# Quantised attention: the maxima lead the exponentials by 18 blocks in place of 24

## The chip, the cores and the metric

The program runs on one NeuronCore of a Trainium2 chip. The metric is the device time of one execution in microseconds. One core has five engines that run their own instruction streams in order and meet by semaphores: TensorE (PE; its weight loads are listed apart as PEld), VectorE (DVE), ScalarE (ACT), GpSimd (POOL) and SyncE (SP), which starts the DMA transfers.

## The reference

Two layers over 2048 tokens of width 256: an attention with quantised operands, a mixture of 32 experts, a time-mixing scan, and a mixture of 8 experts. The change touches the first attention only. It has 16 heads of width 16, and every one of the 2048 queries looks at all 2048 keys:

```python
q = _fq_sym(q, axis=-1)
k = _fq_sym(k, axis=-1)
v = _fq_sym(v, axis=2)
attn = jnp.einsum('bhqd,bhkd->bhqk', q, k)
attn = jax.nn.softmax(attn.astype(jnp.float32), axis=-1)
attn = _fq_unsigned(attn, axis=-1)          # rounded to 0..255 steps of the row's maximum
out = jnp.einsum('bhqk,bhkd->bhqd', attn, v)
```

Because the weights are rounded to 255 steps of the row's largest one, the kernel needs the maximum of every row of scores before it can take that row's exponentials.

## The kernel before

The queries are cut into 16 tiles of 128. A tile and a head make one "head" n of 256 in the kernel's counting (`n = 16 t + h`). The scores of a head (128 x 2048) are computed twice: once for the maxima, in four **blocks** of 512 columns (1024 blocks in all, `fill_maxima`, L219), and once for the exponentials, in two **units** of 1024 columns (512 units, `fill_unit`, L233). The work of one head passes through the engines so:

- PE computes its blocks into PSUM banks 0 to 2 (L219). Block b may be written when the reduction of block b - 3 has emptied its bank. DVE takes the maxima (`top`, L425), two blocks and one block in turn, so three blocks are two reductions and six blocks are four.
- After the last block of a **group** of four heads, and one further reduction, DVE joins the maxima of the group (`shift`, L429), and POOL turns them into the biases of these four heads (L519 and L521, `make_biases`).
- PE computes the head's two units (L233); ACT takes the exponentials to bytes (L484), with the head's bias. PE waits until the unit two before has been read.
- SP transposes the bytes by DMA (L512); POOL widens them to bf16 (`weight`, the CAST at L536, one for each head, three buffers).
- PE multiplies them with the values: 16 small matmuls for each head (`sum_values`, L251), the first of which waits for that head's CAST.

The instruction streams are written out by loops. What ties the stages is the order on PE and on POOL. In each turn of PE's loop (`attention_tensor`, L295) stand 6 blocks, 3 units (one and a half heads) and three calls of `sum_values` for up to 9 of its matmuls each. `LEAD` is how many blocks are computed ahead of that loop, so block 24 + 6 i is the first of turn i, and unit 3 i likewise. The sums of head m start when the units of head m + 4 have been issued (one head later for the first head of a tile):

```python
if m >= NHEAD or u < NUNIT and m + BEHIND + (2 if h == 0 else 1) > u // 2:
    return step
```

On POOL the biases of a group stand in front of a CAST: those for heads n + 5 to n + 8 are made just ahead of the CAST of head n, for n = 3, 7, 11 and so on (62 times, n = 3 to 247):

```python
if n % 4 == 3 and n // 4 + 3 < len(group_of):
    make_biases(po, n // 4 + 3)
po.wait_ge(s_turn[n % 3], 16 * (n // 3 + 1))
```

The group of heads n + 5 to n + 8 ends with block 4 n + 35. Before a tile's outputs are taken (`finish_tile`, L412 and L415), DVE waits for the sums of its last head; where this stands among the reductions follows from `LEAD` too (`tile_end`).

Of the kernel before, what the change touches and what calls it, by code (L numbers as in the profile page):

```python
# [25 lines left out]
def program(nc, a, out, stop=None):  # L26
# [30 lines left out]
    with ExitStack() as whole:  # L57
# [9 lines left out]
        def flat(b0, b1):  # L67

            return bank[:, b0:b1, :].rearrange("p b n -> p (b n)")
# [75 lines left out]
        with ExitStack() as attention:  # L145
# [7 lines left out]
            NBLOCK = NTOK // 512  # L153
# [12 lines left out]

            LN255 = float(np.log(255.0))
            LOGS, SILU = "natural_log_exp_and_others", "silu_and_others"
            LEAD, BEHIND, BYTES = 6 * NBLOCK, 4, 4
            unit = [flat(3, 5), flat(5, 7)]  # L170

            s_blk, s_max = sem("score_blocks_for_maximum"), sem("maxima_taken")
# [2554 lines left out]
```

## Time and profile before

| what | value |
|---|---|
| device time, median of 3 runs | 1216.05 us (1213.13 to 1218.44) |
| profiled execution, span from first to last instruction | 1209.5 us |
| PE busy | 1051.1 us (87%) |
| DVE busy | 967.5 us (80%) |
| ACT busy | 889.2 us (74%) |
| POOL busy | 697.8 us (58%) |
| mean granted TensorE clock | 0.976 of full speed |

The times of the runs are whole executions; the profile is one execution, of which only the span is known, 3.6 to 8.9 us less than the three runs. The first 96 us prepare keys, queries and values, the attention loop lies between 96 and 717 us, its end until about 750 us, and the experts and the mixing fill the rest.

### The profile page before, as it was taken

To read this page: it belongs to the slowest core of one execution; us is meant where nothing else is said; L and a number is where in the kernel's file an instruction comes from. 1 tells how busy PE (TensorE), PEld (TensorE's weight loads), DVE (VectorE), ACT (ScalarE), POOL (GpSimd) and SP (SyncE) were. 2 spreads that over 40 slices of the span, in tenths; PEclk is the share of its full clock that TensorE was granted. 3 is DMA by queue.
4 is the path that set the end of the run, shared out by engine and by line. 5 is a ranking of instruction groups with operands and counts; after the bars stand their busy time and mean duration, and the time that the engine had idled before them with its cause. 6 is when DMAs were issued, how large, how long until landed. Compare 5 with 4: busy or idle time off the path is not lost.

```text
span 1209.5 us, 23983 instructions
## 1 busy us (share of the span) xinstructions
PE 1051.1 (87%) x8245; PEld 616.6 (51%) x8360; DVE 967.5 (80%) x1777; ACT 889.2 (74%) x1542; POOL 697.8 (58%) x610
## 2 busy tenths in 40 slices
PE   6958788888888888888888888897999999989995
PEld 4632444444444444444444457654774465547774
DVE  5999899999999999999999988832437888833335
ACT  3657899999999999999999996613543576824440
POOL 3014898788778888888878875445641001653331
PEclk9978999999999999999999998898999999999998
DMA  6686778888888888888767663856938003323326
GB/s 186 105 152 125 150 156 170 166 183 164 163 175 173 161 173 169 167 172 162 151 114 121 108 106 95 229 143 185 274 100 318 1 1 84 131 81 105 102 88 220
DMA packets 388255, 176.36 MB, mean 146 GB/s; under 512 B 329869, under 2 KB 373106, under 8 KB 388136
## 3 DMA queue, kind: packets, MB, share of 16 engines
q1 hardware_dynamic: 381432, 157.84, 59.7%
q0 software_dynamic: 6480, 16.77, 4.1%
q8 instruction: 69, 1.13, 0.4%
q14 instruction: 50, 0.41, 0.1%
q10 hardware_dynamic: 224, 0.20, 0.1%
HBM read 52.70 MB, written 43.59 MB: 80 GB/s over the span
## 4 chain that ended last, share of the span: by engine, by line
PE 46%; DVE 34%; ACT 7%; issue 6%; DMA 3%; POOL 2%; SPq 1%; another core or an unknown queue 0%; POOLq 0%; ACTq 0%; DVEq 0%
DVE top L425 23%; PE bank L219 8%; PE bank L233 8%; ACT weight L484 5%; PE bank L1174 4%; PE bank L2558 4%; PE bank L251 3%; PE bank L1552 3%; PE bank L2574 3%; PE bank L1569 2%; PE bank L1161 2%; PE bank L1153 2%; POOL weight L536 1%; PE bank L269 1%; PE bank L1797 1%
## 5 line engine op out<-in xcount | busy, mean ns | idle before, releaser
L484 ACT ACTIVATE weight<-bank,bias,sq_all 128x1024 uint8<-128x1024 f32 x512 | 610.2, 1201 | 31.7 <-PE bank L233 27.0
L425 DVE TENSOR_REDUCE top<-bank 128x1 f32<-128x512 f32 (+1 forms) x683 | 610.7, 951 | 15.9 <-PE bank L219 4.9
L536 POOL CAST weight<-turned 128x2048 bf16<-128x2048 uint8 x256 | 478.8, 1893 | 43.8 <-PE bank L251 25.1
L233 PE MATMUL bank<-kT,query 128*128 128x512 bf16 x915 | 284.7, 383 | 27.2 <-ACT weight L484 13.1
L251 PEld LDWEIGHTS bank<-v_sb,weight 128*128 128x128 bf16 x4096 | 172.1, 97 | 107.7 <-POOL weight L536 6.2
L219 PE MATMUL bank<-kT,qspace 64*128 64x512 bf16 x687 | 137.9, 394 | 62.2 <-DVE top L425 62.2
L251 PE MATMUL bank<-v_sb,weight 128*128 128x16 bf16 x4096 | 172.7, 170 | 5.1 <-POOL weight L536 4.7
L219 PE MATMUL bank<-kT,query 128*128 128x512 bf16 x331 | 126.7, 383 | 2.1 <-DVE top L425 1.4
L233 PEld LDWEIGHTS bank<-kT,query 128*128 128x128 bf16 x1024 | 60.0, 97 | 104.9 <-ACT weight L484 62.4
L1782 POOL DMA_INDIRECT dispatched_rows<-qspace,put x32 | 38.4, 1199 | 121.5 <-DVE qspace L2335 112.9
L484 ACT ACTIVATION_READ_ACCUMULATOR weight<-bank,bias,sq_all 128x1 f32 x512 | 101.2, 198 | 0.0
L519 POOL TENSOR_TENSOR shift<-shift,nsq_all 128x4 f32<-128x4 f32 (+1 forms) x65 | 13.0, 200 | 127.8 <-DVE shift L429 127.8
L219 PEld LDWEIGHTS bank<-kT,qspace 64*128 64x128 bf16 x687 | 33.4, 93 | 98.6 <-DVE top L425 93.3
L2697 POOL DMA_INDIRECT answered_rows<-yrow,target x39 | 37.9, 972 | 68.2 <-ACT yrow L2624 62.7
L2656 DVE TENSOR_TENSOR eh<-esil,bank 128x176 f32<-128x176 f32 x39 | 13.2, 338 | 60.8 <-ACT esil L2617 59.3
L219 PEld LDWEIGHTS bank<-kT,query 128*128 128x128 bf16 x337 | 32.7, 97 | 55.6 <-DVE top L425 36.5
L1637 DVE TENSOR_TENSOR qspace<-qspace,bank 128x176 f32<-128x176 f32 x32 | 10.8, 337 | 57.6 <-ACT qspace L1598 36.5
L2558 PE MATMUL bank<-late,erowT 128*128 x156 | 52.6, 460 | 0.0
L1672 POOL DMA_INDIRECT answered_rows<-yrow,target x32 | 31.8, 994 | 33.0 <-issue 15.3
L1174 PE MATMUL bank<-sw,hT 128*128 128x256 f32 x192 | 47.5, 392 | 0.9 <-issue 0.9
L1161 PE MATMUL bank<-xT,sw 128*128 128x512 f32 (+1 forms) x96 | 45.8, 599 | 1.1 <-DVE hT L1194 1.1
L1153 PE MATMUL bank<-xT,sw 128*128 128x512 f32 (+1 forms) x96 | 46.1, 603 | 0.7 <-ACT sil L1184 0.7
(346 smaller groups left out, 1471.3 us busy)
## 6 DMA issues: line engine op xcount, KB each, us to landing
dispatched_rows<-zeros SPq DMA_DIRECT2D x32, 524.0 KB, 3.2
answered_rows<-zeros SPq DMA_DIRECT2D x16, 512.0 KB, 3.1
late<-answered_rows SPq DMA_DIRECT2D x16, 512.0 KB, 6.3
erow<-dispatched_rows SPq DMA_DIRECT2D x39, 131.0 KB
wgu<-in_L_ffn_w_gate SPq DMA_DIRECT2D x26, 176.0 KB
wgu<-in_L_ffn_w_up SPq DMA_DIRECT2D x26, 176.0 KB
wdn<-in_L_ffn_w_down SPq DMA_DIRECT2D x26, 176.0 KB
query<-qspace SPq DMA_DIRECT2D x32, 128.0 KB, 3.1
```

The lines of the kernel that those rows point to most:

```text
L219: pe.matmul(bank[:, k, :], q, kT[rows, h // 2, kb * 512:(kb + 1) * 512], start=True, stop=True).then_inc(s_blk, 1)
L233: mm = pe.matmul(unit[u % 2][:, v * 512:(v + 1) * 512], query2[:, t % 2, h, :], kT[:, h // 2, first + v * 512:first + (v + 1) * 512], star ...
L251: mm = pe.matmul(bank[:, 7, h * HD:(h + 1) * HD], weight[:, m % 3, r // 2, :, r % 2], v_sb[:, r, h * HD:(h + 1) * HD], start=(r == 0), sto ...
L425: ve.tensor_reduce(top[:, first:first + count], bank[:, first % 3:first % 3 + count, :], AX.X, ALU.max).then_inc(s_max, 1)
L484: ac.activation(weight8[:, n % BYTES, u * 1024:(u + 1) * 1024], unit[u], ACT.Exp, bias=bias[:, n:n + 1], scale=sq_all[:, n:n + 1], accum_o ...
L536: po.tensor_copy(weight[:, n % 3, :, :, :].rearrange("p c q two -> p (c q two)"), turned8[:, n % 3, :, :].rearrange("p c q -> p (c q)").bi ...
L1153: mm = pe.matmul(bank[0:w, 0, :], swg[:, k, c * P:c * P + w], xT[:, k, g * 512:(g + 1) * 512], start=k == 0, stop=k == CK - 1)
L1161: mm = pe.matmul(bank[0:w, 1, :], swu[:, k, c * P:c * P + w], xT[:, k, g * 512:(g + 1) * 512], start=k == 0, stop=k == CK - 1)
L1174: mm = pe.matmul(bank[:, 6 + k % 2, 0:C], hT[0:w, c, k * P:(k + 1) * P], swd[0:w, c, :], start=c == 0, stop=c == NW0 - 1)
L1782: po.indirect_dma_start(out=dispatched1, out_offset=bass.IndirectOffsetOnAxis(ap=put1[:, t, k:k + 1], axis=0), in_=rows0[:, t, 0:ROW1], in ...
L2558: mm = pe.matmul(bank[:, 2 + b % 2, 0:2 * F1], erowT1[:, b % 2, k, :], w1gu[:, expert[b], k, :], start=k == 0, stop=k == CK - 1)
L2697: po.indirect_dma_start(out=answered1, out_offset=bass.IndirectOffsetOnAxis(ap=target1[:, b:b + 1], axis=0), in_=yrow1[:, b % YRING, :], i ...
```

## The change

One number: the lead of the maxima falls from 24 blocks (six heads) to 18 (four and a half heads). The instructions are the same in number on every engine.

```diff
-            LEAD, BEHIND, BYTES = 6 * NBLOCK, 4, 4
+            LEAD, BEHIND, BYTES = 9 * NBLOCK // 2, 4, 4
```

`LEAD` sets three things: how many blocks PE computes ahead of its loop (`fill_maxima(pe, 0, LEAD)`), which blocks stand in each turn of the loop, and behind which reduction DVE finishes a tile.

On PE, at the entry of the attention loop (L219 are blocks, a row without a count is one; L233 the two matmuls of a unit; L251 the sums), the rows of the kernel before are these, from block 17 on:

```order
L219 MATMUL bank<-kT,query 128x512
L219 MATMUL bank<-kT,qspace 128x512 x2
L219 MATMUL bank<-kT,query 128x512
L219 MATMUL bank<-kT,qspace 128x512 x2
L219 MATMUL bank<-kT,query 128x512
L219 MATMUL bank<-kT,qspace 128x512 x2
L233 MATMUL bank<-kT,query 128x512 x2
L219 MATMUL bank<-kT,query 128x512
L219 MATMUL bank<-kT,qspace 128x512 x2
L233 MATMUL bank<-kT,query 128x512 x2
```

and these are the rows of the changed kernel, from block 17 on too:

```order
L219 MATMUL bank<-kT,query 128x512
L219 MATMUL bank<-kT,qspace 128x512 x2
L233 MATMUL bank<-kT,query 128x512 x2
L219 MATMUL bank<-kT,query 128x512
L219 MATMUL bank<-kT,qspace 128x512 x2
L233 MATMUL bank<-kT,query 128x512 x2
L219 MATMUL bank<-kT,query 128x512
L233 MATMUL bank<-kT,query 128x512 x2
L219 MATMUL bank<-kT,qspace 128x512 x2
L233 MATMUL bank<-kT,query 128x512 x2
```

The first unit stands behind blocks 18 and 19 in place of 24 and 25: from here to the end each unit, and with it each sum, stands six blocks nearer to the front of the stream of blocks. The turns themselves read alike; what is different is which blocks stand in them. The loop has 168 turns in place of 167, and 8 units are left when it ends, in place of 11.

On DVE, at the end of the first tile, the rows of the kernel before run from the join of a group (L429: the biases of heads 20 to 23, which POOL makes ahead of the CAST of head 15) to the finishing of tile 0 (L412, L415), which needs the sums of head 15:

```order
L429 TENSOR_REDUCE shift<-top 128x4
L425 TENSOR_REDUCE top<-bank 128x1
L425 TENSOR_REDUCE top<-bank 128x2
L425 TENSOR_REDUCE top<-bank 128x1
L425 TENSOR_REDUCE top<-bank 128x2
L425 TENSOR_REDUCE top<-bank 128x1
L425 TENSOR_REDUCE top<-bank 128x2
L425 TENSOR_REDUCE top<-bank 128x1
L425 TENSOR_REDUCE top<-bank 128x2
L412 RECIPROCAL rnorm<-rnorm 128x16
L415 TENSOR_TENSOR late<-bank,rnorm 128x256
```

and in the changed kernel:

```order
L429 TENSOR_REDUCE shift<-top 128x4
L425 TENSOR_REDUCE top<-bank 128x1
L425 TENSOR_REDUCE top<-bank 128x2
L425 TENSOR_REDUCE top<-bank 128x1
L425 TENSOR_REDUCE top<-bank 128x2
L412 RECIPROCAL rnorm<-rnorm 128x16
L415 TENSOR_TENSOR late<-bank,rnorm 128x256
```

Between the join and the point at which the sums of head 15 are needed stand four reductions (six blocks) in place of eight (twelve blocks).

## Rows read from the trace of the kernel before

**Rows 1.** Busy time of each engine by stretch, with the granted clock (PEclk).
```profile
140.00:700.00 560.00, 484.69 (x5332) 253.41 (x5433) 547.41 (x689) 547.59 (x905) 455.70 (x360) 1.00 0.81 158
...
758.60:761.90 3.30, 3.30 (x14) 2.85 (x15) 2.25 (x8) 2.44 (x6) 2.94 (x5) 0.50 1.16 253
772.30:775.60 3.30, 3.06 (x22) 2.87 (x20) 2.11 (x4) 2.99 (x6) 2.11 (x4) 0.50 0.58 164
```

**Rows 2.** Groups of instructions, 150 to 700 us: count, busy, mean ns, idle before.
```profile
L425 DVE TENSOR_REDUCE top<-bank 128x2 f32<-128x1024 f32 x595 | 532.3, 952 | 10.3 <-PE bank L219 0.9
L484 ACT ACTIVATE weight<-bank,bias,sq_all 128x1024 uint8<-128x1024 f32 x446 | 531.4, 1200 | 10.9 <-PE bank L233 6.7
```

**Rows 3.** Who waited for whom, 150 to 700 us: total, times, longest.
```profile
PEld bank L219 <- DVE top L425: 98.8, 314, 1.0
POOL shift L519 <- DVE shift L429: 70.4, 54, 2.3
...
DVE top L425 <- PE bank L219: 0.9, 3, 0.4
PEld bank L251 <- POOL weight L536: 0.8, 1, 0.8
```

**Rows 4.** Timeline of DVE: the join that precedes the CAST of head 139.
```profile
451.20 0.16 DVE L429 TENSOR_REDUCE shift<-top 128x4 f32<-128x16 f32 x1
```

**Rows 5.** Timeline of POOL: biases, and the CASTs from heads 135, 139, 143, 147.
```profile
442.31 5.56 POOL L536 CAST weight<-turned 128x2048 bf16<-128x2048 uint8 x3
...
451.44 0.20 POOL L519 TENSOR_TENSOR shift<-shift,nsq_all 128x4 f32<-128x4 f32 x1 [1.23 <-DVE shift L429]
...
452.01 7.40 POOL L536 CAST weight<-turned 128x2048 bf16<-128x2048 uint8 x4
...
461.17 1.89 POOL L536 CAST weight<-turned 128x2048 bf16<-128x2048 uint8 x1
...
471.93 3.72 POOL L536 CAST weight<-turned 128x2048 bf16<-128x2048 uint8 x2
```

**Rows 6.** Weight loads of the sums of heads 135, 139, 143, 147.
```profile
444.39 0.49 PEld L251 LDWEIGHTS bank<-v_sb,weight 128*128 128x128 bf16 x9
...
454.01 0.49 PEld L251 LDWEIGHTS bank<-v_sb,weight 128*128 128x128 bf16 x9
...
464.30 0.49 PEld L251 LDWEIGHTS bank<-v_sb,weight 128*128 128x128 bf16 x9
...
475.70 0.49 PEld L251 LDWEIGHTS bank<-v_sb,weight 128*128 128x128 bf16 x9
```

**Rows 7.** Timeline of PE around its two waits for a CAST.
```profile
131.99 0.38 PE L251 MATMUL bank<-v_sb,weight 128*128 128x16 bf16 x9 [1.63 <-POOL weight L536]
132.31 0.39 PE L219 MATMUL bank<-kT,qspace 64*128 64x512 bf16 x2
132.63 0.61 PE L233 MATMUL bank<-kT,query 128*128 128x512 bf16 x2
133.07 0.38 PE L219 MATMUL bank<-kT,query 128*128 128x512 bf16 x1
...
142.87 0.38 PE L251 MATMUL bank<-v_sb,weight 128*128 128x16 bf16 x9 [1.53 <-POOL weight L536]
```

**Rows 8.** Timeline of DVE behind the same two waits.
```profile
132.76 9.11 DVE L425 TENSOR_REDUCE top<-bank 128x2 f32<-128x1024 f32 x10 [1.25 <-PE bank L219]
143.65 1.22 DVE L425 TENSOR_REDUCE top<-bank 128x2 f32<-128x1024 f32 x1 [1.77 <-PE bank L219]
```

**Rows 9.** Timeline of PE after the attention: the longest waits from 752 to 776 us.
```profile
758.60 0.29 PE L1272 MATMUL bank<-qspace,before 128*128 128x128 bf16 x1 [4.07 <-DVE qspace L1422]
...
772.00 1.75 PE L280 MATMUL bank<-ident,qspace 128*128 128x128 f32 x8 [1.99 <-ACT qspace L1344]
```

**Rows 10.** Timeline of PE in the loop's first turn, at clock 0.50.
```profile
97.81 1.03 PE L233 MATMUL bank<-kT,query 128*128 128x512 bf16 x2
...
98.64 0.63 PE L219 MATMUL bank<-kT,query 128*128 128x512 bf16 x1
```

## The prediction

> **What bounds the kernel now.** The busy time by stretch comes first: from 140 to 700 us, which is the attention loop, DVE is busy 547.4 and ACT 547.6 of 560 us at a granted clock of 1.00 [rows 1]. So the loop runs at the pace of two full engines, and any time in which DVE stands still is added to the end. The groups of instructions give the pace: 595 reductions in the 550 us from 150 to 700 us are 0.924 us each, so a turn of the loop (6 blocks, four reductions) takes 3.70 us [rows 2]. ACT needs 3 x 1.2 = 3.6 us for the same turn. The list of waits shows how the others hang on this: PE waits for DVE 314 times, 0.31 us on average, DVE waits for PE 0.9 us in all, and PE waits for a CAST only once [rows 3]. The reader should note one more of them: POOL waits for the join of a group 54 times, 70.4 us in all. That is 1.3 us in nearly every group. POOL is the engine that makes the biases and then, behind them in its queue, the CASTs. So the time of the CASTs is already set by the maxima, not by the transposes. The reader is to see a chain: last block of a group, its reduction and the next one, join, biases, CAST, sums.
>
> **The links of that chain.** For head 139 the join begins at 451.20 [rows 4], POOL's first step at 451.44 and the CAST at 452.01. Four CASTs in a row take 7.40 us, 1.85 us each, and one alone 1.89 [rows 5], so that of head 139 ends at 453.90. The weight load for its first sum stands at 454.01, 0.11 us later [rows 6]. From the join to the first sum the chain needs 451.20 to 454.01 = 2.81 us, and PE arrived just in time. For heads 135, 143 and 147, the CASTs begin at 442.31, 461.17 and 471.93 and end 1.89 us later (rows 5 again: the first of each run). Their first sums are the sixth load in the row at 444.39 (nine loads in 0.49 us, so about 444.69), the first in that at 464.30, and the sixth in that at 475.70 (475.97) [rows 6]. That leaves 0.49, 1.24 and 2.15 us. The slack behind the CAST is thus 0.49, 0.11, 1.24 and 2.15 us in four successive groups, 1.0 us on average. (Turns of 1.5 heads, groups of 4 and tiles of 16 come round again every 48 heads, so the other groups repeat such values.)
>
> **The change part by part.** Nothing is added or removed: the same blocks, units, sums, CASTs and DMAs. What moves is every unit and every sum, 6 blocks towards the front. Six blocks are one turn, 3.70 us of DVE's time. Maxima, join, biases and CASTs of a group keep their place in time, because DVE sets it; PE comes to the sums 3.70 us earlier. Of this the slack takes 1.0 us and 0.11 us is the latency from CAST to load, so PE waits at the sums of head n = 3, 7, 11, ... for 3.70 + 0.11 - 1.0 = 2.8 us. In the four groups it is 3.3, 3.7, 2.6 and 1.7 us. It comes 62 times, once for each group whose biases stand ahead of a CAST in the loop.
>
> What is queued behind the waiting load: PE's units (ACT waits for them) and the next blocks (DVE waits). The three banks of maxima can hide little, since PE stands only 2 to 6 blocks behind the group's last block when it stops, and one or two of those are needed for the join itself. The trace has this very wait twice, early on, where POOL is late for another reason: PE waits 1.63 and 1.53 us for a CAST [rows 7], and DVE then stands idle 1.25 and 1.77 us [rows 8]. So 3.16 us of PE's waiting became 3.02 us of DVE's. From the new wait I take off the 0.3 us that PE would have spent waiting for DVE just behind it (98.8 us in 314 waits, rows 3): 2.8 - 0.3 = 2.5 us a group. The bounds are 2.8 (nothing hidden, as the second of the two shows) and 2.2 (two such waits absorbed). **62 x 2.5 = 155 us**, with 136 and 174 as ends.
>
> The later CASTs of the group don't stop PE again: they follow at 1.89 us each, while the sums of a head come every 3.70 / 1.5 = 2.47 us. ACT's biases are ready before the CAST that PE waits for, so ACT waits no longer than PE. SP's transposes hang on the CAST before them and move with it. In the tile's end DVE finishes a tile four reductions behind the join in place of eight; it needs the sums that PE has been waiting for, and by then PE has issued them, so this is the same wait and is not counted twice.
>
> Gains: the first unit comes 6 blocks sooner, but ACT's start doesn't set the end, since DVE has the same reductions to do. Behind the last maximum 8 units are left in place of 11; at 1.2 us each [rows 2] that is at most 3.6 us. I take **-3 us**.
>
> **The clock.** PE's new waits are long enough to ask what its clock does. The trace shows the two waits of 1.63 and 1.53 us inside a loop that keeps 1.00; behind the attention, waits of 4.07 and 1.99 us [rows 9] are each followed by a stretch at 0.50, that is 1.2 in place of 2.4 GHz, of at least 3.3 us [rows 1]. The new waits of 1.7 to 3.7 us lie between and beyond these. The price: a unit's two matmuls take 97.81 to 98.64 = 0.83 us at 0.50 [rows 10] and 132.63 to 133.07 = 0.44 us at 1.00 [rows 7], so a 512-column matmul costs 0.195 us more. A turn has ten in a row (six for units, two blocks, and two pairs of half-height blocks that run side by side). Its time on PE is at full clock, from the starts of [rows 7], two pairs of 0.32, two blocks of 0.22, three units of 0.44 and 24 sums in calls of 8 to 9 at 0.32: 3.25 us. At half clock it is 3.25 + 1.95 = 5.2 us, and PE becomes the bound. In 3.5 us at half clock it does 0.67 of a turn where DVE could do 0.95, which loses 0.28 x 3.70 = 1.0 us. If most groups have one such stretch, some two, and those with short waits none, the term is about 0.7 us a group: **+42 us**; the ends are 0 and 62 x 1.5 = 93 us.
>
> The Trainium skill bears on this: its page "TensorE: Matmul & The Clock Gate", section "HAM oscillation — how this bites in real kernels", says that a wait that returns in every turn of a loop can drop TensorE's clock each time, so that each burst begins at half rate. By that rule all 62 groups pay the 1.0 us, and an estimate by it is 1209.5 + 155 + 62 - 3 + 6.5 = 1430 us; by the two waits that the loop shows, none does. The trace neither confirms nor refutes it for this loop, which has no wait as long.
>
> **The sum.** 1209.5 + 155 + 42 - 3 = 1403.5 us for the span of the profiled execution; the median of the runs lies 6.5 us above that span, so 1410 us.
>
> **The rivals.**
> - *Waits alone, the clock stays at 1.00.* For it: the waits of 1.63 and 1.53 us left the clock alone [rows 1, 7]. Against it: half of the new ones are twice as long. 1209.5 + 155 - 3 + 6.5 = 1368 us (1349 to 1387 with the ends).
> - *The loss is half as big.* PE needs 3.25 us a turn where DVE needs 3.70, so between two waits (2.67 turns) it could gain 1.2 us. If the banks let it use that, 62 x (2.5 - 1.2) = 81 us remain: 1294 us. Against it: three banks allow no run ahead, and DVE's idle time isn't recovered by a faster PE.
> - *The clock falls and stays down.* If a loop that runs at half clock is not active enough to rise again, 168 turns of 5.2 us in place of 3.70 add 252 us, and the waits part of theirs: 1209.5 + 252 + 62 x 1.5 + 6.5 = about 1560 us. For it: no row shows this loop, with its sums, rise from half clock. Against it: its first turn ran at 0.50 [rows 10], and later turns at 1.00 [rows 1].
> - *Not slower.* If PE's sums had 3.8 us of slack behind the CAST, or if POOL made the biases without delaying a CAST, nothing would wait, and only the shorter end would show: 1216 - 3 = 1213 us. It decides at a slack of 3.8 us; the largest of the four is 2.15 [rows 5, 6], and POOL's waits for the join [rows 3] say that the maxima are late already.
>
> **How the numbers follow.** Waits with a falling clock 0.50, waits alone 0.31, half the loss 0.09, clock down for good 0.06, not slower 0.04. The predicted time is that of the first, 1410 us; its own range is 1368 (no group falls) to 1480. The range reaches from the lower end of the second, 1349, to the upper end of the first, 1209.5 + 174 + 93 - 3 + 6.5 = 1480, with 4 and 10 us more for the spread of the runs (1213 to 1218) and for what lies around the span: 1345 to 1490. It leaves out the last three, 0.19 together. About 0.5%, 6 us, is what a measurement of this kernel can tell from no change; the last rival is split between faster 0.015 and within 0.5% 0.025, all others are slower by more: 0.96.
>
> **What would show it.** In the changed profile: some 60 waits of PE's load at L251 for POOL's CAST, 1.6 to 3.7 us each, some 170 us in all; DVE's wait for PE at L425 grown from 0.9 to about 150 us; POOL's wait for the join grown from 1.3 to about 4 us a group; the time between joins 12 to 13 us in place of 9.9 (2.67 turns of 3.70); the loop's granted clock below 1.00. It is wrong if the waits at L251 stay rare, if DVE's idle time per group is far from PE's wait, or if the clock in the loop stays at 1.00 (then 1368 us).

## The result, and the profile after

| | before | lead 18 |
|---|---|---|
| device time, median | 1214.62 us (1213.13 to 1218.44, 4 runs) | 1418.14 us (1414.61 to 1419.81, 4 runs) |
| ratio | 1 | 1.166, 95% interval 1.1637 to 1.1683 |
| span of the profiled execution | 1209.5 us | 1412.9 us |
| mean granted TensorE clock | 0.976 | 0.910 |

The changed kernel is 16.6% slower; 1410 us were forecast. The profiled execution of the changed kernel took 1414.61 us, 1.7 us more than its span.

The costliest groups of the page of the changed kernel, in the form of [rows 2] (count, busy, mean ns, idle before and what ended most of it), here for the whole span:

```profile
L425 DVE TENSOR_REDUCE top<-bank 128x1 f32<-128x512 f32 (+1 forms) x683 | 619.4, 952 | 202.0 <-PE bank L219 186.6
L484 ACT ACTIVATE weight<-bank,bias,sq_all 128x1024 uint8<-128x1024 f32 x512 | 611.8, 1200 | 208.5 <-PE bank L233 195.0
...
L251 PEld LDWEIGHTS bank<-v_sb,weight 128*128 128x128 bf16 x4096 | 180.9, 100 | 293.2 <-POOL weight L536 173.4
...
L519 POOL TENSOR_TENSOR shift<-shift,nsq_all 128x4 f32<-128x4 f32 (+1 forms) x65 | 12.9, 199 | 347.8 <-DVE shift L429 347.8
```

The instructions cost what they did before (952 and 1200 ns); the idle time in front of them is new. DVE and ACT both wait for PE, 186.6 and 195.0 us, PE waits 173.4 us for CASTs, and POOL 347.8 us for joins. The list of waits of the changed kernel, 150 to 850 us, gives the counts that answer to [rows 3]:

```profile
POOL shift L519 <- DVE shift L429: 262.4, 54, 6.5
DVE top L425 <- PE bank L219: 162.9, 89, 3.6
...
PEld bank L251 <- POOL weight L536: 149.1, 63, 3.7
...
PEld bank L219 <- DVE top L425: 76.3, 222, 1.1
```

PE waits for a CAST 63 times, in place of once in a stretch with about as many heads. Read head by head in the trace, 53 of the 63 belong to heads 3, 7, 11, ...: 2.7 us on average, 3.7 at most. Of the ten others eight are under 0.3 us. One of the long ones, in the timelines of the changed kernel's DVE, POOL and PEld (head 111, the last of its tile):

```profile
468.30 0.16 DVE L429 TENSOR_REDUCE shift<-top 128x4 f32<-128x16 f32 x1
468.37 0.68 DVE L425 TENSOR_REDUCE top<-bank 128x1 f32<-128x512 f32 x1
471.83 1.82 DVE L425 TENSOR_REDUCE top<-bank 128x2 f32<-128x1024 f32 x2 [2.78 <-PE bank L219]
```

```profile
468.54 0.20 POOL L519 TENSOR_TENSOR shift<-shift,nsq_all 128x4 f32<-128x4 f32 x1 [5.50 <-DVE shift L429]
468.83 0.22 POOL L521 TENSOR_SCALAR bias<-shift 128x4 f32<-128x4 f32 x1
469.11 1.89 POOL L536 CAST weight<-turned 128x2048 bf16<-128x2048 uint8 x1
```

```profile
471.05 0.29 PEld L251 LDWEIGHTS bank<-v_sb,weight 128*128 128x128 bf16 x9 [3.60 <-POOL weight L536]
```

Join at 468.30, CAST from 469.11 to 471.00, first load at 471.05: 2.75 us from join to load, as in [rows 4 to 6]. But PE had stood there for 3.60 us, while in the kernel before its load for head 139 came 0.11 us behind the end of the CAST [rows 5, 6]. DVE had one reduction left (0.68 us) and then nothing for 2.78 us.

The stretches of the changed kernel (busy time of each engine, then the granted clock, as in [rows 1]): the loop, the time just behind this wait, and the 10 us after that:

```profile
150.00:850.00 700.00, 513.21 (x5001) 250.51 (x5094) 524.00 (x651) 526.71 (x854) 423.61 (x337) 0.89 0.60 120
472.20:475.40 3.20, 3.19 (x15) 0.86 (x14) 2.36 (x3) 2.59 (x4) 3.20 (x3) 0.50 0.80 154
475.60:485.60 10.00, 7.37 (x81) 3.81 (x82) 8.49 (x14) 8.58 (x14) 4.19 (x5) 1.00 0.42 103
```

From about 1 us behind the wait of 3.60 us the clock stands at 0.50, and PE is busy all the time; then it is back at 1.00. Over the loop it is 0.89: (1 - 0.89) x 700 / 0.5 = 154 of these 700 us run at half clock. In the whole loop a stretch at 0.50 follows 41 of the 62 waits of heads 3, 7, 11, ...: 1 of the 13 waits under 1.6 us, 35 of the 41 over 2.3 us.

How long the loop takes is read from the joins (first and last start, behind the durations), in the changed kernel

```profile
L429 DVE TENSOR_REDUCE shift<-top x65: 149/159/170, 85.6 to 911.4; 128x4 f32<-128x16 f32 x63, 128x2 f32<-128x8 f32 x2
```

and in the kernel before from 85.9 to 716.6. The last join comes 194.8 us later; the 64 distances between joins are 12.9 us on average in place of 9.9. What follows the last join takes 1412.9 - 911.4 = 501.5 us in place of 492.9.

### The profile page after: what moved, and what is told of

It is laid out like the page before. It is cut to its first block, busy times and chain, and to the rows that moved or that the text cites. A ratio compares the mean times of both kernels' runs of the same rounds, so it can differ in the third digit from the quotient of the medians.

```text
span 1412.9 us, 23984 instructions
## 1 busy us (share of the span) xinstructions
PE 1127.0 (80%) x8246; PEld 638.8 (45%) x8360; DVE 974.7 (69%) x1777; ACT 901.6 (64%) x1542; POOL 694.3 (49%) x610
## 4 chain that ended last, share of the span: by engine, by line
PE 51%; DVE 24%; POOL 11%; issue 6%; ACT 4%; DMA 3%; SPq 1%; another core or an unknown queue 0%; POOLq 0%; DVEq 0%; ACTq 0%
DVE top L425 17%; PE bank L233 11%; PE bank L219 10%; POOL weight L536 9%; PE bank L251 5%; PE bank L2558 3%; PE bank L1174 3%; PE bank L1552 3%; PE bank L2574 2%; PE bank L1569 2%; PE bank L1161 2%; PE bank L1153 2%; PE bank L269 1%; ACT weight L484 1%; POOL shift L519 1%
## 5 line engine op out<-in xcount | busy, mean ns | idle before, releaser
L425 DVE TENSOR_REDUCE top<-bank 128x1 f32<-128x512 f32 (+1 forms) x683 | 619.4, 952 | 202.0 <-PE bank L219 186.6
L484 ACT ACTIVATE weight<-bank,bias,sq_all 128x1024 uint8<-128x1024 f32 x512 | 611.8, 1200 | 208.5 <-PE bank L233 195.0
L233 PE MATMUL bank<-kT,query 128*128 128x512 bf16 x915 | 321.3, 427 | 22.9 <-issue 10.1
L251 PEld LDWEIGHTS bank<-v_sb,weight 128*128 128x128 bf16 x4096 | 180.9, 100 | 293.2 <-POOL weight L536 173.4
L251 PE MATMUL bank<-v_sb,weight 128*128 128x16 bf16 x4096 | 183.5, 171 | 153.5 <-POOL weight L536 152.5
L219 PE MATMUL bank<-kT,qspace 64*128 64x512 bf16 x687 | 152.1, 435 | 48.4 <-DVE top L425 47.4
L519 POOL TENSOR_TENSOR shift<-shift,nsq_all 128x4 f32<-128x4 f32 (+1 forms) x65 | 12.9, 199 | 347.8 <-DVE shift L429 347.8
L219 PE MATMUL bank<-kT,query 128*128 128x512 bf16 x332 | 141.6, 426 | 2.1 <-DVE top L425 1.1
L233 PEld LDWEIGHTS bank<-kT,query 128*128 128x128 bf16 x1024 | 62.5, 99 | 108.1 <-issue 69.8
L219 PEld LDWEIGHTS bank<-kT,qspace 64*128 64x128 bf16 x687 | 34.0, 94 | 85.3 <-DVE top L425 79.0
L219 PEld LDWEIGHTS bank<-kT,query 128*128 128x128 bf16 x337 | 36.2, 108 | 60.3 <-DVE top L425 27.3
```

Of the source, the lines that this page charges most:

```text
L219: pe.matmul(bank[:, k, :], q, kT[rows, h // 2, kb * 512:(kb + 1) * 512], start=True, stop=True).then_inc(s_blk, 1)
L233: mm = pe.matmul(unit[u % 2][:, v * 512:(v + 1) * 512], query2[:, t % 2, h, :], kT[:, h // 2, first + v * 512:first + (v + 1) * 512], star ...
L251: mm = pe.matmul(bank[:, 7, h * HD:(h + 1) * HD], weight[:, m % 3, r // 2, :, r % 2], v_sb[:, r, h * HD:(h + 1) * HD], start=(r == 0), sto ...
L425: ve.tensor_reduce(top[:, first:first + count], bank[:, first % 3:first % 3 + count, :], AX.X, ALU.max).then_inc(s_max, 1)
L484: ac.activation(weight8[:, n % BYTES, u * 1024:(u + 1) * 1024], unit[u], ACT.Exp, bias=bias[:, n:n + 1], scale=sq_all[:, n:n + 1], accum_o ...
```

## The experiments

Two theories stood against each other at first. **A**, that of the forecast: PE stands at the sums of heads 3, 7, 11, ... because their CAST is queued on POOL behind biases that wait for the join, and DVE starves behind PE; the clock adds its part. **B**: a lead of four and a half heads is too short in itself, since the exponentials need the biases, wherever POOL makes them. All ratios are to the kernel before, measured on the same chip.

### Biases behind one CAST, and behind two, at lead 18

```diff
-                    if n % 4 == 3 and n // 4 + 3 < len(group_of):
-                        make_biases(po, n // 4 + 3)
                     po.wait_ge(s_turn[n % 3], 16 * (n // 3 + 1))
...
                     po.tensor_copy(weight[:, n % 3, :, :, :].rearrange("p c q two -> p (c q two)"),
                                    turned8[:, n % 3, :, :].rearrange("p c q -> p (c q)").bitcast(U8)).then_inc(s_wide, 1)
+                    if n % 4 == 3 and n // 4 + 3 < len(group_of):
+                        make_biases(po, n // 4 + 3)
```

In the second kernel the two added lines make the same biases one CAST later:

```diff
+                    if n >= 4 and n % 4 == 0 and n // 4 + 2 < len(group_of):
+                        make_biases(po, n // 4 + 2)
```

> Lead 18, and on POOL the biases of a group stand behind the CAST of head n (n = 3, 7, ...) in place of ahead of it; PE, DVE and ACT streams as in the changed kernel. Theory A (PE waits because a CAST is queued behind biases that wait for the join): the CAST of head n is no longer held up, only that of head n+1, which PE needs one head (2.47 us) later, so of the wait of 3.8 us minus slack only what exceeds 2.47 us is left: 0.8, 1.2, 0.1, 0 us in four groups, about 0.3 us of DVE's time a group after the 0.3 us that it would have waited anyhow: 62 x 0.3 = 20 us, about 1235 us, clock in the loop near 1.00. Rival B (a lead of 18 is too short in itself: ACT's exponentials wait for the biases, wherever POOL makes them): stays at 1400 us or more, with ACT's wait for POOL at L484 where PE's wait at L251 was.

> Lead 18, biases behind the CAST of head n+1 as well, so two CASTs are no longer held up. Theory A: nothing is left of PE's wait (3.8 us less than 2 x 2.47 us): 1212 to 1220 us. Rival B: 1400 us or more, ACT waiting for biases.

Measured: 1232.69 us behind one CAST, ratio 1.015 (1.010 to 1.0199), and 1215.79 us behind two, ratio 0.9996 (0.998 to 1.0012). The streams of PE, DVE and ACT are those of the changed kernel. Moving two instructions of 0.2 us for each group, behind one CAST and then behind two in POOL's queue, takes back first 185 and then all of the 203 us. The waits of the first kernel, 150 to 700 us:

```profile
PEld bank L251 <- POOL weight L534: 22.1, 33, 1.9
```

and of the second:

```profile
DVE top L425 <- PE bank L219: 3.9, 10, 0.8
ACT weight L484 <- POOL bias L521: 3.0, 8, 1.0
```

Behind one CAST PE still waits 33 times, now mostly for the CAST of the next head and for 0.7 us on average. Behind two, one wait of PE for a CAST is left in this list, 0.8 us, as in the kernel before [rows 3], and ACT's waits for a bias begin to show: 8 of them, 3.0 us in all. So B falls: a lead of 18 is long enough for the exponentials, barely, and the 203 us were due to what stood behind the biases in POOL's queue.

### Joins four reductions later at lead 24

```diff
-                if r - 1 in group_end:
-                    n0, k = group_end[r - 1]
-                    ve.wait_ge(s_max, r)
+                if r - 5 in group_end:
+                    n0, k = group_end[r - 5]
+                    ve.wait_ge(s_max, min(r, NRED))
...
-                for r in range(last_reduction(LEAD - 1) + 1, NRED + 1):
+                for r in range(last_reduction(LEAD - 1) + 1, NRED + 5):
```

> Lead 24 as before, but DVE joins each group four reductions (six blocks, 3.70 us) later than it could; nothing else is moved, so the entry of the loop, its 167 turns and the 11 units at its end are those of before. Theory A (the distance from the join to the first sum behind it is the whole cause): as slow as the changed kernel, 1405 to 1430 us. Rival F (part of the loss comes from what else the lead sets: the entry, the end of the loop, where a tile is finished): clearly below 1418 us, by the share that these have.

Measured: 1415.22 us, ratio 1.164 (1.1623 to 1.1657), against 1.166 (1.1637 to 1.1683) for lead 18. The lead is that of before, and only the distance from the join to the sums is that of the changed kernel. The waits, 150 to 850 us, read like those of the changed kernel too:

```profile
POOL shift L519 <- DVE shift L429: 260.9, 53, 6.7
...
DVE top L425 <- PE bank L219: 167.6, 92, 3.6
PEld bank L251 <- POOL weight L536: 152.1, 61, 3.7
```

A holds, and F falls: what else the lead sets (entry, end) adds nothing that can be measured. DVE finishes a tile four reductions behind the join in this kernel as well; but so it does in the second kernel above, which is as fast as the kernel before, so this place alone costs nothing.

### Joins one reduction sooner at lead 18

```diff
-                if r - 1 in group_end:
-                    n0, k = group_end[r - 1]
-                    ve.wait_ge(s_max, r)
+                if r in group_end:
+                    n0, k = group_end[r]
+                    ve.wait_ge(s_max, r + 1)
```

> Lead 18, and DVE joins a group right behind its last reduction in place of one reduction later (0.92 us sooner). Theory A: each of the 62 waits is shorter by what the join is earlier, 0.92 us less up to 0.2 us in which DVE waits for its own last result: 62 x 0.7 to 0.9 = 45 to 55 us, and some of the falls of the clock go with the longest waits (10 to 20 us): 1345 to 1365 us. Rival G (what counts is only that POOL's biases stand in front of the CAST, not when the join comes): 1418 us.

Measured: 1356.44 us, ratio 1.1143 (1.1124 to 1.1162): 62 us less than lead 18 (1418.14 us) for 0.92 us at each of 62 joins. In the changed kernel's list above 63 waits for a CAST come to 149.1 us; in this kernel's, over the same 700 us,

```profile
PEld bank L251 <- POOL weight L536: 122.3, 76, 3.2
```

The counts can't be compared as they stand: this stretch holds more heads, since the loop is faster, and more short waits of other heads. At the 62 heads 3, 7, 11, ... themselves the wait is 1.95 us on average in place of 2.69, 0.73 us less, or 45 us together, and the longest is 0.5 us shorter. The other 17 of the 62 us are left for the clock, 0.931 of full speed in place of 0.910 over the profiled execution (10 to 20 us were expected of it). That only the order on POOL counts and not the time of the join (G) falls.

### Lead 21

```diff
-            LEAD, BEHIND, BYTES = 9 * NBLOCK // 2, 4, 4
+            LEAD, BEHIND, BYTES = 21, 4, 4
```

> Lead 21. Theory A: the sums move by three blocks, 1.85 us, so PE waits 1.96 us minus the slack: 1.5, 1.85, 0.7 and 0 us in four groups, 1.0 us on average, and 0.7 us after what PE would have waited for DVE anyhow: 62 x 0.7 = 45 us, no clock falls: about 1260 us. Rival D (the loss goes in proportion to the lead taken away): half of 203 us, 1317 us. Rival E (a threshold: the wait starts only below a lead of 20): 1216 us.

Measured: 1268.44 us, ratio 1.0426 (1.0404 to 1.0449). In its list of waits from 96 to 770 us, PE's for a CAST are

```profile
PEld bank L251 <- POOL weight L536: 66.7, 61, 2.1
...
DVE top L425 <- PE bank L219: 53.5, 59, 2.0
```

about 1.1 us each in this list. At the 62 heads 3, 7, 11, ... alone it is 0.9 us on average, against 1.0 expected. Half of the cut in the lead (3 blocks in place of 6) costs a quarter of the loss: the slack of up to 2.15 us behind each CAST [rows 5, 6] is spent first, and the clock falls little, to 0.98 over this stretch, where no fall was expected. So neither proportion (D) nor threshold (E) fits, and the forecast's sum over the groups does.

### PE kept busy in the waits, lead 18

```diff
+                        if m % 4 == 3:
+                            for _ in range(16):
+                                pe.matmul(bank[:, 7, 256:512], kT[:, 0, 0:128], kT[:, 0, 0:256], start=True, stop=True)
                         pe.wait_ge(s_wide, m + 1)
```

> The changed kernel, and ahead of each wait for a CAST at n = 3, 7, ... PE computes 16 matmuls of 256 columns into an unused part of bank 7 (1.7 us at full clock, which lie inside waits of 1.6 to 3.7 us). The output is unaffected. Theory A with a clock term: the waits last as long as before in time, but PE stands idle for only what is left of them, the clock falls in fewer groups, and the time falls from 1418 us by up to the clock term of about 40 us: 1375 to 1395 us, granted clock of the loop 0.97 or more in place of 0.89. Rival C (the low clock costs nothing, since it lies under waits): 1418 us or a little more with the clock at 0.97.

Measured: 1378.18 us, ratio 1.1342 (1.1305 to 1.138). PE does more and the kernel is 40 us faster than the changed one. Its loop, in the form of [rows 1]:

```profile
150.00:850.00 700.00, 587.25 (x6135) 336.04 (x6244) 541.98 (x678) 545.81 (x891) 446.10 (x352) 0.98 0.63 124
```

and its waits for a CAST over the same stretch:

```profile
PEld bank L254 <- POOL weight L539: 63.6, 67, 2.3
```

The clock is 0.98 in place of 0.89, and the joins run

```profile
L432 DVE TENSOR_REDUCE shift<-top x65: 150/159/170, 86.1 to 878.0; 128x4 f32<-128x16 f32 x63, 128x2 f32<-128x8 f32 x2
```

to 878.0 in place of 911.4 us. PE stops for about as long as before, since nothing in the chain is moved: from the first useless matmul to the first load of the sums it is 2.60 us on average at the 62 heads, against waits of 2.69 us in the changed kernel. But it works for most of that time. So the low clock costs time of its own, beside the waits: 33 us of the loop at least, a little low clock being left. C falls.

### Lead 24 with the biases behind two CASTs, and with the bias rows in small pieces

The first kernel is the kernel before with the edit on POOL of the second kernel above. The second has this besides:

```diff
-                    if n in (9, 13, 17, 21):
-                        g = (n - 9) // 4
-                        po.tensor_tensor(x_sb[:, g * G:(g + 1) * G, :], x_sb[:, g * G:(g + 1) * G, :], bp_all[:].unsqueeze(1).broadcast_to([P, G, C]), ALU.add)
+                    if 9 <= n < 9 + NT:
+                        g = n - 9
+                        po.tensor_tensor(x_sb[:, g, :], x_sb[:, g, :], bp_all[:], ALU.add)
```

> Lead 24 as before, with the biases behind two CASTs, as in the run with lead 18. Theory A: at lead 24 DVE stands still for PE about 5 us in all, of which 3 us come from the two early waits for a CAST; these get shorter, the rest is DVE's own work: 1211 to 1216 us, within 0.5% of the kernel before. Rival: POOL's 1.3 us wait for each join costs something at lead 24 too: 1200 us or less.

> The same, and POOL adds the output bias to the rows in 16 pieces of one tile, one behind each of 16 CASTs, in place of four pieces of 2.35 us: the two early waits for a CAST go, 3 us of DVE's idle time: 1209 to 1214 us. Rival (16 small pieces cost POOL more than four large ones, and the waits come back): 1216 us.

Measured: 1217.20 us, ratio 1.0011 (0.9995 to 1.0027), and 1218.62 us, ratio 1.0015 (1.0003 to 1.0028). POOL's 1.3 us wait for each join is gone in both (one of 10 us at the loop's entry is left) and the time is the same: it cost nothing at lead 24. The second was expected to be 2 to 7 us faster and isn't. PE's early waits for a CAST went as meant (none from 96 to 720 us), but the biases now come behind more work in POOL's queue, and in their place stands, over the same stretch,

```profile
ACT weight L484 <- POOL bias L521: 6.7, 11, 1.3
```

DVE's wait for PE is 7.8 us there and 7.6 us in the first kernel, where it was 4.9 before: the small pieces moved a wait and did not remove it.

### Lead 30

```diff
-            LEAD, BEHIND, BYTES = 9 * NBLOCK // 2, 4, 4
+            LEAD, BEHIND, BYTES = 30, 4, 4
```

> Lead 30, everything else as in the changed kernel (biases ahead of the CAST). Theory A: the slack behind the CAST grows by 3.70 us, no PE wait for a CAST is left after the two early ones or with them; POOL waits less for the joins; DVE has the same reductions: 1210 to 1217 us, within 0.5% of the kernel before. Rival (more lead shortens the loop further, since POOL's 1.3 us wait for each join at lead 24 still cost something): 1200 us or less.

Measured: 1221.58 us, ratio 1.0057 (1.0035 to 1.008): a little slower, which neither side expected. Its joins and its sums (first and last start):

```profile
L429 DVE TENSOR_REDUCE shift<-top x65: 148/159/170, 86.2 to 718.9; 128x4 f32<-128x16 f32 x63, 128x2 f32<-128x8 f32 x2
```

```profile
L251 PE MATMUL bank<-v_sb,weight x4096: 169/169/221, 114.5 to 753.2; 128*128 128x16 bf16 x196
```

The last sum starts 753.2 - 718.9 = 34.3 us behind the last join, where it is 745.7 - 716.6 = 29.1 us in the kernel before. The loop leaves 14 units behind the last block in place of 11, and the last exponential starts 744.9 - 718.9 = 26.0 us behind the last join in place of 21.6, so these units come later too. Of the 7.5 us between the two profiled spans (1217.0 and 1209.5) these 5.2 us lie in the end and 2.3 us ahead of the last join. That the three units more are the cause is argued from this; no run moves them alone.

## Why the prediction was right, step by step

- **The chain from the join to the sums.** Forecast 2.81 us, measured 2.75 us in the head shown and on average. PE was to come 3.70 us sooner and wait at 62 heads, for 1.6 to 3.7 us: it waits at all 62, for 1.2 to 3.7 us. In heads 135, 139, 143 and 147, for which 3.3, 3.7, 2.6 and 1.7 us were forecast, the changed kernel has

```profile
548.83 0.19 PEld L251 LDWEIGHTS bank<-v_sb,weight 128*128 128x128 bf16 x5 [3.17 <-POOL weight L536]
562.16 0.32 PEld L251 LDWEIGHTS bank<-v_sb,weight 128*128 128x128 bf16 x9 [3.70 <-POOL weight L536]
576.39 0.29 PEld L251 LDWEIGHTS bank<-v_sb,weight 128*128 128x128 bf16 x9 [2.52 <-POOL weight L536]
589.84 0.22 PEld L251 LDWEIGHTS bank<-v_sb,weight 128*128 128x128 bf16 x6 [1.50 <-POOL weight L536]
```

  The two kernels that move only the joins, and the two that move only the biases on POOL, show that this chain is the cause.
- **The size of the waits.** Forecast 62 x 2.5 = 155 us of DVE's time, without the clock. The kernel with PE kept busy is nearest to that case: its loop is 878.0 - 716.6 = 161.4 us longer, with some low clock left in it. PE's mean wait at the 62 heads is 2.69 us (166.5 us together), against the forecast 2.8.
- **The clock.** Forecast +42 us; keeping PE busy takes back 1418.14 - 1378.18 = 40 us, with a little low clock left. The rule of the Trainium skill's page "TensorE: Matmul & The Clock Gate", section "HAM oscillation — how this bites in real kernels", that a returning wait can drop the clock again and again, agrees with the loop's 0.89. Its sum of 1430 us, in which all 62 groups pay, was 12 us too long; the clock fell behind 41 of the 62 waits. That a fallen clock would stay down is refuted by the stretch from 475.6 us on.
- **Together** the loop: forecast +197 us, measured +194.8 us.
- **The end, forecast at -3 us.** This term had the wrong sign: the part behind the last join is 501.5 us in place of 492.9. Up to the last sum it takes 942.5 - 911.4 = 31.1 us in place of 29.1. In the kernel with the biases behind two CASTs, where no wait disturbs it, the last exponential starts 734.9 - 717.7 = 17.2 us behind the last join in place of 738.2 - 716.6 = 21.6 us, but the last sum 746.8 - 717.7 = 29.1 us, as before. So the three units fewer do end sooner, and the sums behind them don't. The other 6.6 of the 8.6 us lie behind the last sum, in instructions that the change doesn't touch. From there to the end, the kernel before, the changed kernel and the one with the biases behind two CASTs show (in the form of [rows 1])

```profile
745.70:1209.50 463.80, 420.84 (x1856) 273.65 (x1852) 263.20 (x832) 216.11 (x449) 165.34 (x172) 0.96 0.45 138
942.50:1412.90 470.40, 431.53 (x1854) 280.49 (x1850) 263.71 (x831) 215.77 (x450) 165.27 (x172) 0.94 0.44 137
746.80:1217.90 471.10, 431.17 (x1856) 279.50 (x1852) 263.64 (x831) 214.79 (x450) 165.28 (x172) 0.94 0.44 136
```

  DVE, ACT and POOL are busy as long in all three; PE is busy longer, at a lower granted clock. The third kernel is as fast as the kernel before in the median, so nothing here ties these 6.6 us to the lead. Over all eleven profiled executions this part takes 463.6 to 467.6 us where the clock is 0.96 (six of them) and 469.2 to 471.1 us where it is 0.94 (three). Why the clock there differs between executions stays open.
- **From the span to the median** the forecast added 6.5 us; it is 5.2 us for the changed kernel. The three errors (2 us less in the loop, 12 us more behind it, 1 us less around it) make up the 8 us between 1410 and 1418.
- **The rivals.** *Waits alone* falls with the loop's clock of 0.89 and the 40 us that keeping PE busy takes back. *Half the loss* (PE running ahead between waits, +81 us) falls with the +161.4 us of the loop that has little low clock, and *not slower* with the result. POOL's wait for the joins, forecast at about 4 us a group, is 262.4 / 54 = 4.9 us; what made it longer was not tried.

## What to carry to other kernels

When a distance in a software pipeline is shortened, look for what else stands in the in-order queue of the engine that turns the early result into the late one: here the biases could come two CASTs later without loss, but the CAST queued behind them could not. Measure the slack at the point where two streams meet (here 0.1 to 2.2 us behind each CAST) and set it against the shift; the loss begins when the smallest slack is spent, and it grows with each group that follows. Here the busiest engine had no time to spare, and the kernel lost about as much as it waited (161 us of the loop with PE kept busy, for 62 waits of 2.6 us); waits that came round again cost TensorE's clock on top.

## What the runs showed of the hardware that was not expected

Idle time on TensorE can be worth filling with useless matmuls: 16 of them ahead of each wait (1.64 us to the next load where nothing was left to wait for) took 40 us from a kernel of 1418 us, with a granted clock of 0.98 in place of 0.89 in the loop. And a lead 25% longer than that of before cost 0.57% (0.35 to 0.8%), most of it behind the last join.
